# The last addition of a group of samples moved behind the second step of the next, coordinates made beside the next row blocks, and a sigmoid read from PSUM

## The reference

```python
x = x + _L0_conv_ref(_gn(x), ...)   # linear attention in 9 chunks of 1024 tokens, group norm
x = x + _L1_conv_ref(_gn(x), ...)   # offsets by a 3x3 convolution, bilinear samples, 3x3 convolution
x = x + _L2_conv_ref(_gn(x), ...)   # 3x3 convolution
x = x + _L3_conv_ref(_gn(x), ...)   # deformable 3x3 convolution, below
```

```python
sim = _similarity(x)                                  # cosines with 8 neighbours
om = _conv3x3(jnp.concatenate([x, sim], axis=1), cm_weight, cm_bias)
o1, o2, m = jnp.split(om, 3, axis=1)                  # 18 offsets and 9 masks for a pixel
mask = jax.nn.sigmoid(m)
...
y0 = jnp.floor(py); x0 = jnp.floor(px)                # py, px: offsets + pixel + tap
val = g00 * (1 - wy1) * (1 - wx1) + g01 * (1 - wy1) * wx1 + g10 * wy1 * (1 - wx1) + g11 * wy1 * wx1
val = val * mask[:, None]
out = jnp.einsum('bckhw,ock->bohw', val, weight.reshape(weight.shape[0], C, KK))
```

## Time and profile before

| | us |
|---|---|
| median of 3 runs | 9844.04 |
| lowest, highest | 9841.66, 9857.14 |
| span of the profiled execution | 10272.1 |
| stage 2 of it (3719 to 6043) | 2324 |
| stage 4 of it (8368 to 10272) | 1904 |
| VectorE busy | 6423.8 |
| GpSimd busy | 6273.4 |
| TensorE busy | 5575.5 |

### The profile page before, as it was taken

One profiled execution on the slowest core, in us unless ns is written; L12 is line 12 of the kernel. 1 busy time (PEld: TensorE's weight loads), 2 busy tenths in 40 slices (PEclk: granted clock), 3 DMA queues, 4 the chain that ended last, 5 costly groups with the idle time before them and its releaser, 6 DMA issues. The chain is left out here.

```text
span 10272.1 us, 87003 instructions
## 1 busy us (share of the span) xinstructions
PE 5575.5 (54%) x26226; PEld 3400.6 (33%) x26226; DVE 6423.8 (63%) x6965; ACT 2142.2 (21%) x3640; POOL 6273.4 (61%) x5206
## 2 busy tenths in 40 slices
PE   4565766577655656577655645577655632222112
PEld 3332234355422234355422223355522211111111
DVE  5798466799845456799845456699845443333333
ACT  2343412232212112223212212233202200000000
POOL 0000047677766557677766557677767557777777
PEclk9877877788877767788876777788877765555555
DMA  2000223322324333322324323322224323333333
GB/s 67 19 0 19 65 92 97 97 77 78 97 80 122 104 97 96 98 77 76 96 79 122 106 94 94 99 77 78 94 79 123 104 85 97 97 98 97 97 98 88
DMA packets 443186, 887.37 MB, mean 86 GB/s; under 512 B 119072, under 2 KB 268918, under 8 KB 439924
## 3 DMA queue, kind: packets, MB, share of 16 engines
q0 software_dynamic: 248832, 679.81, 22.6%
q1 hardware_dynamic: 190708, 129.65, 4.3%
q10 hardware_dynamic: 3456, 75.50, 1.8%
HBM read 763.04 MB, written 121.53 MB: 86 GB/s over the span
## 5 line engine op out<-in xcount | busy, mean ns | idle before, releaser
L643 POOL DMA_INDIRECT gathered_corners<-gather_table,metas x5184 | 6265.2, 1209 | 3975.3 <-issue 2821.5
L702 DVE TENSOR_TENSOR gathered_corners<-gathered_corners,metas 128x2304 f32<-128x2304 f32 x432 | 1105.3, 2559 | 1774.4 <-DMA gathered_corners<-gather_table,metas 1705.3
L1364 PE MATMUL ps<-ident,sampled 128*128 128x128 f32 (+1 forms) x2160 | 496.8, 384 | 2570.7 <-DVE sampled L707 2517.6
L1123 ACT COPY sampled_by_channel<-ps 128x512 f32<-128x512 f32 x576 | 336.6, 584 | 4687.9 <-PE ps L1364 2912.1
L1364 PEld LDWEIGHTS ps<-ident,sampled 128*128 128x128 f32 (+1 forms) x2160 | 331.1, 186 | 2793.3 <-issue 2478.5
L1435 PE MATMUL ps<-region,woff 128*128 (+1 forms) x3456 | 1181.5, 498 | 23.6 <-ACT region L1108 23.6
L1361 PE MATMUL ps<-ident,weighted_corners 128*128 128x128 f32 (+1 forms) x5760 | 852.4, 316 | 253.9 <-DVE weighted_corners L700 252.1
L1361 PEld LDWEIGHTS ps<-ident,weighted_corners 128*128 128x128 f32 (+1 forms) x5760 | 808.1, 219 | 338.5 <-issue 206.4
L1435 PEld LDWEIGHTS ps<-region,woff 128*128 128x128 f32 x3456 | 654.2, 192 | 499.2 <-issue 48.6
L1348 PE MATMUL ps<-sampled_by_channel,w 128*64 128x256 f32 x2880 | 706.5, 461 | 32.8 <-ACT sampled_by_channel L1124 21.2
L876 DVE TENSOR_TENSOR work<-work 128x768 f32<-128x768 f32 x720 | 667.2, 956 | 5.0
(11 more groups left out here) (224 smaller groups left out, 7358.9 us busy)
## 6 DMA issues: line engine op xcount, KB each, us to landing
gathered_corners<-gather_table,metas POOLq DMA_INDIRECT x5184
x_after_layer<-region ACTq DMA_DIRECT2D x8, 4608.0 KB, 12.8
gather_table<-tabst SPq DMA_DIRECT2D x192, 192.0 KB
region<-in_x_dram ACTq DMA_DIRECT2D x12, 1536.0 KB, 9.6
region<-x_after_layer ACTq DMA_DIRECT2D x4, 4608.0 KB, 15.5
res<-x_after_layer SPq DMA_DIRECT2D x144, 128.0 KB
out_dram<-ob SPq DMA_DIRECT2D x144, 128.0 KB
indices_and_weights<-region SPq DMA_DIRECT2D x16, 810.0 KB
```

The source lines that it names most:

```text
L643: pool.indirect_dma_start(out=G[:, s % NG, k, :], out_offset=None, in_=table, in_offset=bass.IndirectOffsetOnAxis(ap=idx[:, s * KK + k:s * ...
L702: ch.own(ch.after().tensor_tensor(Gs, Gs, w.unsqueeze(2).to_broadcast([128, 4 * KK, C]), ALU.mult))
L1364: mm = pe.transpose(out_m, V[:, s % 2, 128 * m:min(128 * m + 128, KK * C)], ident[:, :])
```

## The change

The addition of group g is taken out of the end of the group and put behind the second step of group g+1 (on VectorE alone; the tables lose their `None`). On SyncE the order for a group becomes: next indices, store of the group before, residual of this one. In the offsets TensorE and ScalarE take one step after each pair; the last three steps stand behind all pairs. The coordinates of a part are cut in two pieces, which stand after steps of the next group (`META_PLACES`). ScalarE reads the masks from PSUM, two sigmoids for each pair (128x54 each), into `masks`; the copy L1063 and its handshake go. The load of the next x is put ahead of the last three steps. The first chunk and the first group of stage 4 are written out ahead of their loops.

```diff
-CONV_PLACES = ((0,), (1, 2), (3, None))
+CONV_PLACES = ((0,), (1, 2), (3,))
...
-OFFSET_PLACES = ((0, 1), (2,), (3,))
+OFFSET_PLACES = (((0, 0), (0, 1)), ((0, 2),), ((0, 3),), ((1, 0),), ((1, 1),), ((1, 2),), ((1, 3),),
+                 ((2, 0),), ((2, 1),), ((2, 2),), ((2, 3),), ((3, 0),), ((3, 1), (3, 2), (3, 3)))
+
+META_PLACES = {(1, 0): ((0, 0),), (1, 1): ((0, 1),), (1, 3): ((1, 0),), (2, 0): ((1, 1),), (2, 2): ((2, 0),), (2, 3): ((2, 1),),
+               (3, 1): ((3, 0),), (3, 2): ((3, 1),)}
...
-                def group(g, e, last=False):
-                    load_res(g)
+                def group(g, e, first=False, last=False):
                     if not last:
                         sp.wait_ge(weighted, g * STEPS + CREDIT)
                         load_meta(g + 1, 1 - e)
-                    store_out(g)
+                    if not first:
+                        store_out(g - 1)
+                    load_res(g)
...
-                        if sample and u == 0 and h > 0:
-                            store_out(g - 1)
-                            load_res(g)
-                            if g + 1 < GROUPS:
-                                sp.wait_ge(weighted, g * STEPS + CREDIT)
-                                load_meta(g + 1, (g + 1) % 2)
...
+                    load_cosines(q, q % 2)
+                    if sample and q in (3, 7):
+                        g = G_OFFSETS + (q + 1) // 4
+                        sp.wait_ge(weighted, g * STEPS + CREDIT)
+                        load_meta(g + 1, (g + 1) % 2)
+                    if sample and q in (6, 10):
+                        g = G_OFFSETS + (q + 1) // 4
+                        store_out(g - 1)
+                        load_res(g)
...
                         for s in steps:
-                            if s is None:
-                                finish(g)
-                            else:
-                                weigh(g, slot, s, sum_on_pe)
+                            weigh(g, slot, s, sum_on_pe)
+                            if s == 1 and not first:
+                                finish(g - 1)
...
+                def coordinates(h):
+                    v.wait_ge(om_tcp, (h + 1) * (PAIRS // PARTS) + 2)
...
+                for h in range(PARTS):
+                    for s in ((2, 3) if h == 0 else (0, 1, 2, 3)):
+                        steps_of(h + G_OFFSETS, (h + G_OFFSETS) % 2, (s,), False)
+                        for part, piece in META_PLACES.get((h, s), ()):
+                            (coordinates, corner_weights)[piece](part)
                     ch.restart()
+                if sample:
+                    finish(GROUPS - 1)
...
                 def kept(q, e):
                     act.wait_ge(om_tr, q + 3)
-                    nc.scalar.copy(omT[:, bass.ds(q * 6, 6), :].rearrange("p (h a) j -> p h a j", h=2),
-                                   ps[:, 2 + e, 0:3 * 128].rearrange("p (a h j) -> p h a j", a=3, h=2)[:, :, :, 0:54]).then_inc(om_tcp, 1)
...
+                    turned_om = ps[:, 2 + e, 0:3 * 128].rearrange("p (a h j) -> p h a j", a=3, h=2)
+                    for h in range(2):
+                        t0 = q * 6 + h * 3
+                        nc.scalar.activation(masks[:, t0:t0 + 3], turned_om[:, h, :, 0:54].rearrange("p a (i c) -> p a i c", i=2)[:, :, :, 18:27],
+                                             ACT.Sigmoid)
+                    nc.scalar.copy(omT[:, bass.ds(q * 6, 6), :].rearrange("p (h a) j -> p h a j", h=2), turned_om[:, :, :, 0:54]).then_inc(om_tcp, 1)
...
+                act.wait_ge(x3_stored, 16)
+                offset_steps(0)
                 biased(0, 0)
                 for q in range(PAIRS):
...
                     if q > 0:
-                        steps_of(h + G_OFFSETS, OFFSET_PLACES[u])
-                    if ahead and q == PAIRS - 1:
-                        act.wait_ge(om_mm, PAIRS + 2)
-                        load_x(p + 1)
-                    if u == PAIRS // PARTS - 1:
-                        mask(h)
+                        offset_steps(q)
+                if ahead:
+                    act.wait_ge(om_mm, PAIRS + 2)
+                    load_x(p + 1)
+                offset_steps(PAIRS)
```

More of the change, by code:

```diff
@@ L249, in build @@
         M = TILES // PARTS * 2 * KK
-        coordinate_slots = [R1[:, q * M:(q + 1) * M] for q in range(7)]
-        meta_all = R1[:, 7 * M:7 * M + GROUPS * META]
+        coordinate_slots = [R1[:, q * M:(q + 1) * M] for q in range(6)]
+        masks = R1[:, 6 * M:6 * M + TILES * 2 * KK].rearrange("p (t i k) -> p t i k", i=2, k=KK)
+        meta_all = R1[:, 10 * M:10 * M + GROUPS * META]
         norm2 = T[0:PIECES, 8000 + 8 * CUT:8000 + 18 * CUT]
@@ L516, in group @@
                         load_meta(g + 1, 1 - e)
-                    store_out(g)
+                    if not first:
+                        store_out(g - 1)
+                    load_res(g)
                 if sample:
                     load_meta(0, 0)
+                    group(0, 0, first=True)
+                    group(1, 1)
                     ahead = G_COSINES if prepare else GROUPS - 2
-                    with sp.Fori(0, ahead // 2) as j:
+                    with sp.Fori(1, ahead // 2) as j:
                         for e in range(2):
@@ L526, in _ @@
                     group(GROUPS - 2, 0)
-                    group(GROUPS - 1, 1, True)
+                    group(GROUPS - 1, 1, last=True)
+                    store_out(GROUPS - 1)
                     sp.wait_ge(out_stored, 16 * (GROUPS + 1))
@@ L733, in _ @@
                 if not prepare:
-                    with v.Fori(0, GROUPS) as g:
-                        steps_of(g, g % 2, (0, 1, 2, 3, None), False)
+                    steps_of(0, 0, (0, 1, 2, 3), False, first=True)
+                    ch.restart()
+                    with v.Fori(1, GROUPS) as g:
+                        steps_of(g, g % 2, (0, 1, 2, 3), False)
                         ch.restart()
+                    finish(GROUPS - 1)
+                    ch.restart()
                     return
@@ L754, in stage, with chunk @@
                               staged, c + 1)
-                def chunk(c, last):
+                def chunk(c, first=False, last=False):
                     slot = c % 2
-                    steps_of(c, slot, (0,), False)
+                    steps_of(c, slot, (0,), False, first)
                     for i in range(2):
@@ L808, in _ @@
                 ch.restart()
-                with v.Fori(0, NCHUNK - 1) as c:
-                    chunk(c, False)
-                chunk(NCHUNK - 1, True)
+                chunk(0, first=True)
+                with v.Fori(1, NCHUNK - 1) as c:
+                    chunk(c)
+                chunk(NCHUNK - 1, last=True)
                 group_norm(1, 18, EPS, affine=True)
@@ L1055, in _ @@
                 slots = [a.rearrange("p (t i k) -> p t i k", t=PT, i=2) for a in coordinate_slots]
-                py, px, fl, q1, q2, mk, idx = slots
-                for h in range(PARTS):
-                    steps_of(h + G_OFFSETS, (h + G_OFFSETS) % 2, (2, 3) if h == 0 else (0, 1, 2, 3), False)
-                    v.wait_ge(om_tcp, h * (PAIRS // PARTS) + (PAIRS // PARTS + 2))
-                    sig = omT[:, bass.ds(h * PT, PT), :].rearrange("p t (i c) -> p t i c", i=2)
-                    meta = meta_all[:, bass.ds(h * (PG * META), PG * META)].rearrange("p (g m) -> p g m", m=META)
-                    half = lambda a: a.rearrange("p (g a) i k -> p g (a i k)", a=2)
-                    ch.named(ch.after().tensor_copy(mk, sig[:, :, :, 18:27]), sig_in, h + 1)
+                py, px, fl, q1, q2, idx = slots
@@ L1065, in _ @@
                         for i in range(2):
[L1066 removed]
+                            ch.own(ch.after().tensor_tensor(z[:, :, i, :], sig[:, :, i, c0:18:2], base[:, h * PT:(h + 1) * PT, :], ALU.add))
                         ch.own(ch.after().tensor_scalar(z, z, -1.0, float(HW), ALU.max, ALU.min))
[L1069 to L1079 removed]
+                    floor_of(py)
@@ new lines, in coordinates, with floor_of @@
+                    ch.own(ch.after().tensor_scalar(idx, fl, float(TAB_W), first_row[:, :], ALU.mult, ALU.add))
+                def floor_of(z):
+                    ch.own(ch.after().tensor_copy(q1.bitcast(I32), z))
+                    ch.own(ch.after().tensor_copy(fl, q1.bitcast(I32)))
+                    ch.own(ch.after().tensor_tensor(q2, fl, z, ALU.is_gt))
+                    ch.own(ch.after().tensor_tensor(fl, fl, q2, ALU.subtract))
+                    ch.own(ch.after().tensor_tensor(z, z, fl, ALU.subtract))
@@ L1518, in _, with offset_steps @@
                 pe.wait_ge(cos_cp, RT + 2)
+                def offset_steps(q):
+                    for h, s in OFFSET_PLACES[q]:
+                        steps_of(h + G_OFFSETS, (s,), False)
                 def offsets_and_mask(q, e):
```

78 lines of the change are left out of this document (35 added, 43 removed).

## The result

The changed kernel takes 9682.44 us (median of 4 runs, 9675.86 to 9688.13), the kernel before 9844.29 (4 runs, 9841.66 to 9857.14). The ratio is 0.9834, 95% interval 0.9821 to 0.9847: 162 us less, where 171 were forecast.

The account below looks back on a forecast made before the run. GpSimd's gathers were taken as the stages' floor, VectorE as the tap products' bound. Taps 18.5 + seams 14.7 + offsets 24 = 57 us in each of stages 1 to 3; 9844 - 171 = 9673 us, own range 9610 to 9724.

Parts of the forecast that it names:

- the lateness: Late signals before additions and offsets, read as the profiled execution's own; its span is 428 us longer than the runs' median.
- rival 1: Lateness real in every run: convolution gives 52, seams 35.8 instead of 14.7; about 9454 us; chance 0.13.
- Tap products: VectorE is the bound there, so moving the addition saves its whole wait for TensorE, 18.5 us a stage.
- Seams: Three places where a VectorE chain follows the addition at once: 4.9 us each, 14.7 a stage, at most 35.8.
- Convolution: A group's 51.1 us of gathers covers the addition's wait of some 7 us: 0; other bound some 52 us.
- Offsets: One step per pair, coordinates beside gathers: 20 us first part, 7 last, less 3: 24 a stage; bounds 7 and 96.0.
- The stop of the first part: In the offsets GpSimd stands some 20 us while VectorE waits for the first part's third pair; that time goes.
- the 8 that the prediction had set as a sign: Expected in the profile after: no wait over 8 us for the first part's offsets.
- VectorE beside gathers: Each microsecond of VectorE work beside gathers costs them 0.29 us; 2 of the 3 us taken off the offsets.
- Rival 2: Coordinates block the gathers fully, 13.8 us for 13.8 in three parts: 19 us a stage left, 9787 us; chance 0.09.
- Sigmoid: Two ScalarE activations a pair from PSUM, covered by a 13 us step: 0; uncovered, 8 us a stage.
- Rivals 3 and 4: 3: nothing waited for the addition, gathers set offsets, 9823 us, chance 0.06; 4: TensorE bounds the offsets, 9990, chance 0.08.

## Why the prediction was right, and where it was not

**The whole.** 9673 forecast, 9682 measured; 57 us a stage forecast, 48 in the profiles.

**Reading the lateness as the first profile's own** decided it. The 73 us a stage of rival 1 aren't there: the second profile of the kernel before has the span of the runs, and the additions of its convolution wait 7 us each.

**Tap products**: 18.5 forecast, 16.1 measured, and 17.2 + 6 lost when they and the seam ahead are put back. Before and after, by line:

```profile
L643 POOL DMA_INDIRECT gathered_corners<-gather_table,metas x406 | 583.9, 1438 | 156.4 <-issue 120.4 <-DVE weighted_corners L700 36.0
...
L715 DVE SCALAR_TENSOR_TENSOR ob<-ps,chan,res 128x256 f32<-128x256 f32 x11 | 5.3, 483 | 15.8 <-PE ps L1348 15.8
```

```profile
L654 POOL DMA_INDIRECT gathered_corners<-gather_table,metas x416 | 614.5, 1477 | 126.8 <-issue 126.8
...
L711 DVE TENSOR_TENSOR weighted_corners<-gathered_corners,metas 128x2304 f32<-128x2304 f32 x46 | 117.7, 2558 | 13.4 <-DVE region L919 7.3 <-DVE small L879 3.2 <-DMA gathered_corners<-gather_table,metas 2.9
...
L726 DVE SCALAR_TENSOR_TENSOR ob<-ps,chan,res 128x256 f32<-128x256 f32 x12 | 5.8, 484 | 0.4
```

GpSimd's 36.0 us of waiting for VectorE are gone, a gather takes 1477 ns instead of 1438, and the products L711 wait 2.9 us for gathers. GpSimd, with 614.5 us of gathers and 126.8 between them in a window of 740 us, has no pause left here, and VectorE is busy 703 of the 740; the next wait taken from VectorE should give less, which no run tries.

**Seams**: 14.7 forecast, three times 4.9. The table gives 5.6 at the normalization and 5.4 - 2.8 at the convolution, and the chunks take 1.3 more: 6.9. The run with two of the three back says 0 to 4 us a stage for those two. This step failed. The prediction named what stands behind the addition on VectorE but not what the next instruction there waits for: the same projection, by TensorE's order (4.56 us), and GpSimd's lead, which was used up (5.98 us). It is most of the 9 us by which the stage fell short of the forecast.

**Convolution**: 0 forecast, 0 shown by the run with the additions back.

**Offsets**: 24 forecast, 16.6 + 8.0 = 24.6 measured, and 26 lost when the coordinates go back. The stop of the first part was the term that carried it: VectorE's wait was 22.10 us before and is 8.68 after, GpSimd's was 26.48 and none is above 6.4. The 8.68 us, alike in all three stages, are more than the 8 that the prediction had set as a sign; with a step weighed ahead of them they no longer stop GpSimd as before. What I had not seen is that neither half of the change gets the term alone.

**VectorE beside gathers**: the price of 0.29 us for a microsecond, worked out from the means of two stretches, was wrong by some four times for instructions as short as the coordinates'. Its sum was off a little as well: VectorE works 727.68 / 48 = 15.2 us a step in the taps and 690.53 / 144 = 4.8 in stage 4, 10.4 us more and not 8.9, which gives 0.25. In the sum it stood for 2 of 57 us, so little came of it: in the offsets a gather takes 1139 ns before and 1177 or 1151 in the two profiles of the changed kernel (mean of three stages), 2 to 5 us a stage for 126 gathers. Rival 2 (13.8 for 13.8) falls with it: the short products beside the gathers cost 0.07. The Trainium skill, "SBUF — State Buffer", section "SBUF: two separate sides", describes the lock for VectorE instructions in a two-port mode, or with two inputs in SBUF against a GpSimd instruction that reads SBUF. The 2.66 us gather of the earlier trace rows, beside a product of two inputs, agrees. One for one was the prediction's reading of it, and it doesn't hold here for short products, which have two inputs as well.

**Sigmoid**: 0 forecast, 0 to 9 us measured.

**Rivals 3 and 4** are refuted: the tap products' waits were on the path, and TensorE's rows don't crawl in the changed kernel. Its timeline of TensorE in the offsets, an early pair and the longest stretch of 36 rows:

```profile
5472.90 6.03 PE L1555 MATMUL ps<-region,wcm 128*64 128x384 f32 x36
...
5568.86 8.01 PE L1555 MATMUL ps<-region,wcm 128*64 128x384 f32 x36
```

## What to carry to other kernels

A wait at the end of a piece of work is worth its price where the waiting engine is the bound (the tap products). Where a chain on it follows, look first at what the next instruction waits for: an engine that works in order may wait there for the same thing, or soon behind it for another engine, as at two of the three seams. Two changes around one stop can be worth little or less than nothing one by one and work together, as long as either leaves something to wait for ahead of the next useful instruction. Where a profile's span differs from the runs by more than their spread, take a second profile before pricing its waits.

## What the runs showed of the hardware

One profiled execution of a kernel was 4.5% longer than another (10272.1 against 9834.3 us) at the same granted clock (0.743 and 0.741), with an addition that waited 20.5 us and started 7.7 us after the last matmul of its projection, and matmul rows beside gathers 0.5 us apart; what caused it stays open. In stage 4, beside the same gathers, the 2.56 us products of VectorE go with 0.61 us of longer gathers for each of their microseconds, those of 0.50 us with 0.08; 564 us of the short ones added cost 36 to 38 us. The two differ in more than length.
